# Turned attention heads: bank emptied by a ScalarE copy and divided on GpSimd instead of VectorE

## The reference

```python
xn = _layernorm(x, axis=-1)
# attention: q, k with rotary embedding, 4 query heads for each key/value head
scores = jnp.einsum('bqhd,bkhd->bhqk', q, k) / jnp.sqrt(jnp.float32(D))
probs = jax.nn.softmax(scores.astype(jnp.float32), axis=-1)
s = jnp.einsum('bhqk,bkhd->bqhd', probs, v).reshape(B, S, E)
# gate: z + gamma * m with gamma from the norms of z and m (low rank), then silu
g = _silu(z + gamma * m)
x = x + s * g
```

## Time and profile before

| | us |
|---|---|
| median of 3 runs | 461.4 |
| lowest and highest | 460.72 and 463.13 |
| the profiled execution | 464.08 |
| span of the profiled execution | 462.3 |
| PE busy | 449.7 |
| VectorE (DVE) busy | 379.2 |
| ScalarE (ACT) busy | 302.3 |
| GpSimd (POOL) busy | 87.9 |

### The profile page before, as it was taken

How to read it: one execution, slowest core, us unless ns; L and a number is a source line. 1 busy time by engine, 2 the same in 40 slices (tenths; PEclk the granted TensorE clock), 3 DMA queues, 4 the chain that set the end, 5 groups by cost and what they waited for, 6 DMA issues and landing times.

```text
span 462.3 us, 8804 instructions
## 1 busy us (share of the span) xinstructions
PE 449.7 (97%) x3237; PEld 203.6 (44%) x3237; DVE 379.2 (82%) x639; ACT 302.3 (65%) x593; POOL 87.9 (19%) x159
## 2 busy tenths in 40 slices
PE   8898999999999999999999999999999999999995
PEld 3465343443444444444444444444444444433342
DVE  5553588888999999999999999999999999534422
ACT  2120001224888888888888888888888888745594
POOL 8463212434101000000100010010001001014442
PEclk9989599999899999999999999999999999999998
DMA  8979944444000000000000000000000000020011
GB/s 261 319 108 125 114 68 68 68 72 69 2 1 3 1 4 1 1 4 1 3 0 3 3 2 3 1 3 0 3 4 1 3 0 3 2 81 2 20 47 36
DMA packets 13364, 17.45 MB, mean 38 GB/s; under 512 B 3088, under 2 KB 7440, under 8 KB 13328
## 3 DMA queue, kind: packets, MB, share of 16 engines
q1 hardware_dynamic: 11808, 15.84, 18.3%
q10 hardware_dynamic: 1520, 1.12, 0.9%
HBM read 6.72 MB, written 2.10 MB: 19 GB/s over the span
## 4 chain that ended last, share of the span: by engine, by line
PE 88%; DMA 4%; SPq 3%; DVE 2%; ACT 1%; issue 1%; POOL 0%; DVEq 0%
PE st L947 34%; PE oT L901 29%; PE sm L840 8%; PE st L780 7%; PE sm L920 3%; DMA kA<-arena 2%; PE sm L911 2%; DMA idb_sb<-in_identb 2%; PE oT L780 2%; PE st L816 1%; SPq L281 1%; PE sm L923 1%; DVE negmax L638 1%; SPq L313 1%; SPq L287 1%
## 5 line engine op out<-in xcount | busy, mean ns | idle before, releaser
L570 ACT ACTIVATE arena<-st 128x512 f32<-128x512 f32 x512 | 266.9, 600 | 56.5 <-PE st L947 53.5
L646 DVE TENSOR_REDUCE neghalf<-sm 128x1 f32<-128x512 f32 x448 | 270.7, 683 | 2.3 <-PE sm L840 0.4
L840 PE MATMUL sm<-kA,qA 48*128 48x512 f32 x512 | 187.7, 454 | 2.0 <-DMA kA<-arena 1.9
L947 PE MATMUL st<-qA,kA 50*128 50x512 f32 x512 | 177.9, 442 | 1.0 <-ACT arena L570 0.7
L901 PE MATMUL oT<-arena,vg 128*32 128x256 f32 (+3 forms) x1792 | 147.3, 421 | 0.0
L947 PEld LDWEIGHTS st<-qA,kA 50*128 50x128 f32 x512 | 84.2, 185 | 110.7 <-ACT arena L570 87.2
L840 PEld LDWEIGHTS sm<-kA,qA 48*128 48x128 f32 x512 | 85.9, 186 | 23.0 <-issue 14.0
L901 PEld LDWEIGHTS oT<-arena,vg 128*32 128x32 f32 x1792 | 38.7, 108 | 52.7 <-issue 42.2
L638 DVE TENSOR_REDUCE negmax<-sm 128x1 f32<-128x1024 f32 x32 | 38.1, 1221 | 15.9 <-PE sm L840 15.5
L409 POOL TENSOR_TENSOR maxp<-negmax,consts 128x16 bf16<-128x16 f32 x16 | 3.4, 214 | 214.2 <-DVE negmax L653 214.2
L497 ACT ACTIVATE arena<-arena 128x512 fp32r<-128x512 f32 x10 | 6.3, 630 | 57.7 <-POOL arena L369 57.7
(11 more groups left out here) (90 smaller groups left out, 259.6 us busy)
## 6 DMA issues: line engine op xcount, KB each, us to landing
qA<-arena SPq DMA_DIRECT2D x48, 128.0 KB, 5.1
x_sb<-in_x SPq DMA_DIRECT2D x8, 256.0 KB, 5.7
kA<-arena SPq DMA_DIRECT2D x12, 128.0 KB, 6.8
wT_sb<-in_wT SPq DMA_DIRECT2D x1, 1024.0 KB, 9.1
out<-x_sb SPq DMA_DIRECT2D x1, 896.0 KB, 4.0
out<-x_sb SPq DMA_DIRECT2D x4, 224.0 KB, 2.0
z_sb<-in_wq SPq DMA_DIRECT2D x1, 768.0 KB, 10.6
wkv<-in_wk ACTq DMA_DIRECT2D x1, 256.0 KB, 4.1
```

The lines of the kernel that those rows point to most:

```text
L570: act.activation(probs[:, s % PB, h, :], st[:, (st_score(0, s, h) - late) % 3, :], ACT.Exp, scale=float(D) ** -0.5).then_inc(st_free, 1)
L646: dve.tensor_reduce(neghalf[:, e // 16, e % 16, j % 2:j % 2 + 1], sm[:, n % 4, :], AX.X, ALU.max, negate=True).then_inc(sm_free, count)
L840: pe.matmul(sm[:, n % 4, :], qA[rows, half, g // 2, h, qt * P:(qt + 1) * P], kA[rows, g // 2, kh * HALF:(kh + 1) * HALF], start=True, stop ...
L947: pe.matmul(st[:, n % 3, :], kA[rows, g // 2, kt * P:(kt + 1) * P], qA[rows, half, g // 2, h, :], start=True, stop=True).then_inc(st_full, 1)
```

## The change

In groups 0 to 6, ScalarE copies the bank of turned heads into a tile in SBUF (`turned`, the memory of `junk`), ahead of exponential 12 or 44, and adds to a new semaphore `turned_out`. GpSimd makes the reciprocals as a power of -1 and multiplies. VectorE goes from maximum 11 to 12 and from 43 to 44 with nothing between them, and adds two to `sm_free` after maximum 11 and 43, one of them for the bank of turned heads; the matmul that writes this bank next (of pair 15 or 47) waits for `turned_out`. In the last group VectorE goes on as before. ScalarE's groups 1 to 6 are written out.

```diff
+        turned = junk[:, :, :].rearrange("p a n -> p (a n)").bitcast(F32)
...
+            def scale_turned(n, to):
+
+                came = turned.rearrange("p (t h c) -> p t h c", t=TH, h=REP)
+                sums = rsum[:, :].rearrange("p (t h) -> p t h", t=TH)
+                pool.wait_ge(turned_out, n + 1)
+                pool.tensor_tensor(sums, came[:, :, :, D], consts[:, 2:3].unsqueeze(2).broadcast_to((P, TH, REP)),
+                                   ALU.pow).then_inc(sums_inv, 1)
+                pool.wait_ge(sums_inv, n + 1)
+                pool.tensor_tensor(to.rearrange("p t (h d) -> p t h d", h=REP), came[:, :, :, 0:D],
+                                   sums.unsqueeze(3).broadcast_to((P, TH, REP, D)), ALU.mult).then_inc(heads_scaled, 1)
...
             def step(g, first=False):
                 if not first:
                     group_values(g)
+                    scale_turned(2 * g - 1, late_heads[:, :, (g - 1) * (REP * D):g * (REP * D)])
                 maxima(0, 2 * g + 3, 2 * g + 1,
                        (pj_full, PJ_AT["max0", 0] + 1) if first else (st_full, st_max0(g - 1) + 1))
+                scale_turned(2 * g, scaled[:, :, :])
...
+            def copy_turned(n, at):
+
+                act.wait_ge(sm_full, at + 1)
+                act.wait_ge(heads_scaled, n)
+                act.activation(turned, sm[:, at % 4, :], ACT.Copy).then_inc(turned_out, 1)
...
+                        if 4 * s + h == OUT1_AT and not first and not last:
+                            copy_turned(2 * g - 1, sm_out1(g))
+                        if 4 * s + h == OUT0_AT and not last:
+                            copy_turned(2 * g, sm_out0(g))
...
-            with act.Fori(1, LAST) as g:
+            for g in range(1, LAST):
                 step(g)
...
                 for j in range(64):
                     if j == 33:
                         both_halves(g, 0)
-                    if j == OUT1_AT and not first:
-                        hold_heads(g - 1, sm_out1(g), 1)
-                    if j == OUT0_AT:
-                        scale_heads(sm_out0(g), 1, 2 * g, scaled[:, :, :], None if first else g)
-                    row_max(g, j, 2 if first and j == OUT1_AT - 1 else 1)
+                    row_max(g, j, 2 if j in (OUT1_AT - 1, OUT0_AT - 1) else 1)
...
+                    if i == OUT1_AT + 3 and not first and not last:
+                        pe.wait_ge(turned_out, 2 * g)
+                    if i == OUT0_AT + 3 and not last:
+                        pe.wait_ge(turned_out, 2 * g + 1)
```

More of the change, by code:

```diff
@@ L252, in build @@
             "heads_out", "sums_inv", "heads_scaled", "heads_gated", "group_done"))
+        turned_out = sem("turned_out")
         late_copied, late_scaled, late_added = sem("late_copied"), sem("late_scaled"), sem("late_added")
@@ L689, in scale_heads @@
             def scale_heads(at, banks, n, to, done):
-                turned = sm[:, at % 4, :].rearrange("p (t h c) -> p t h c", t=TH, h=REP)
+                bank = sm[:, at % 4, :].rearrange("p (t h c) -> p t h c", t=TH, h=REP)
                 dve.wait_ge(sm_full, at + banks)
+                dve.wait_ge(heads_scaled, n)
                 if done is not None:
                     dve.wait_ge(group_done, done)
-                dve.reciprocal(rsum[:, :].rearrange("p (t h) -> p t h", t=TH), turned[:, :, :, D]).then_inc(sums_inv, 1)
+                dve.reciprocal(rsum[:, :].rearrange("p (t h) -> p t h", t=TH), bank[:, :, :, D]).then_inc(sums_inv, 1)
                 dve.wait_ge(sums_inv, n + 1)
-                dve.tensor_tensor(to.rearrange("p t (h d) -> p t h d", h=REP), turned[:, :, :, 0:D],
+                dve.tensor_tensor(to.rearrange("p t (h d) -> p t h d", h=REP), bank[:, :, :, 0:D],
                                   rsum[:, :].rearrange("p (t h) -> p t h", t=TH).unsqueeze(3)
```

## The result

The changed kernel takes 455.28 us (median of 4 runs, 454.3 to 456.25), the kernel before 461.06 in the same comparison (460.28 to 463.13). The ratio is 0.9868, with a 95% interval of 0.9829 to 0.9907: 5.8 us faster, where 5.7 were forecast. The sum came out; one of its terms did not, as the experiments show.

A forecast was written before the change was run, and what follows sets the result against it. VectorE's chain was taken to bound the loop; earlier maxima gain 6 x (0.43 + 0.44) + 0.46 = 5.7 us, with other costs counted as hidden, taking the 461.4 us median to 455.7 us, range 452.5 to 458.9.

The forecast's parts named there:

- VectorE bounds the loop: Loop of the kernel before: VectorE's chain alone explains the 40.4 us period, though PE and ScalarE are close.
- has almost no hole: VectorE in one loop turn before the change: measured busy 40.10 of 40.5 us, so almost no idle time.
- What is late next: At the turned heads: maximum 12 must wait for pair 12 until 204.50, so 0.43 us gained, 0.48 idle.
- rival 1: VectorE's reciprocals and products: the whole 12.1 us comes back, giving 449.3 us; chance 0.08.
- The period: One loop turn: 39.6 us forecast after the change, with 0.43 and 0.44 us gained at its two places.
- I see neither a gain nor a loss in it: ScalarE's groups 1 to 6 written out instead of looped: counted as no effect on time.
- ScalarE's copy: Copy ahead of exponential 12: falls in ScalarE's idle 0.88 us, delays it 0.06; costed at nothing, 0.8 kept for the range.
- Rivals 2 and 3: ScalarE or PE takes over, 462.1 or 458.9 us, chance 0.12; copy delays exponential 12, 467.8 us, chance 0.04.
- One sign of being wrong: PE's waits for ScalarE's exponentials, 66.9 us before: growth by several us would show the forecast wrong.
- The new wait of PE: PE's matmul of pairs 15 and 47 also waits for the copy: cost zero, with 1.1 us of cover.
- GpSimd: Power of 16 elements 3.2 us and product 0.73 us per turn, hidden in GpSimd's idle time: cost zero.
- rival 4: GpSimd's product comes too late for the next copy: a power of 19.5 us would give 468.7 us; chance 0.01.

## Why the prediction was right

**VectorE bounds the loop.** Right, with a small correction. The kernel before doesn't care where the reciprocal and the product lie (period 40.28 at both places), and the changed one doesn't care how much VectorE does in the gap. But "has almost no hole" was not quite true: about 0.1 us of each gap of 0.91 and 0.96 us was a wait for the turned heads, hidden under the end of a maximum, as the written-out loop shows.

**What is late next.** The step that decided the size was to ask when pair 12 can be reduced, and to read it from the exponential of the same pair. It gave a gap of 1.08 us between maxima 11 and 12 and an idle time of 0.4; measured are 1.05 and 0.36. The full 12.1 us of rival 1 did not come.

**The period.** 0.87 us were forecast for it. The move of the division gave 40.28 - 39.45 = 0.83 and the loop written out 0.19, together 1.01. So the prediction's sentence on ScalarE's written-out loop, "I see neither a gain nor a loss in it", is the step that failed, by 0.19 us a group, 1.1 us in all; the division was over-estimated by 0.04 a group. In the loop the gain is 6.5 us and not 5.7, of which the division is 5.4 (from the first to the last `both_halves` it is 261.25 us with only the loop written out, and 255.90 after the change). That the medians differ by 5.8, within 0.1 us of the forecast, is partly luck: the interval of the ratio, 0.9829 to 0.9907, is a gain of 4.3 to 7.9 us, and holds both, so the medians alone would not have shown the missing term. The failed step rested on exponential 44 alone, which is not late in the hardware loop; the delay of `evacuate` and of exponential 32 shows only beside a kernel with the loop written out.

**ScalarE's copy.** Cost nothing, right: none of 13 x 0.06 us was passed on (39.45 with and without). Rivals 2 and 3 had the price wrong too: even a second copy costs 0.13 and not 0.49 at a place. One sign of being wrong did come in part: PE's waits for exponentials grew by 3.5 us over the loop (66.9 to 70.4). The copies are not the reason, since without them it is 69.9 us, and the loop became shorter all the same.

**The new wait of PE** is nowhere in the view of waits. Right.

**GpSimd.** The power takes 2.91 us where 3.2 were estimated from one and two elements, the product 0.62 where 0.73 was taken. Both are hidden, and so is a second power; rival 4 is far off. The advice of the Trainium skill, "GPSIMD Engine Reference", section "Engine selection", to leave elementwise work on VectorE did not decide here: power and product take 2.91 and 0.62 us on GpSimd, reciprocal and product 0.26 and 0.42 on VectorE, and only VectorE's lay on the path.

## What to carry to other kernels

When the bounding engine is relieved, ask which input it will wait for next, and read the arrival time from another engine that uses the same matmul: this gave the half that was gained and the half that turned into idle time. Then move that input: here two constants took another 4.8 us (455.28 to 450.52; 4.15 of it between the first and the last `both_halves` of the profiles), more than four fifths of what the change itself had brought. And treat a loop in hardware or written out as part of the change: written out it was worth 1.1 us in the kernel before, and a hardware loop with two groups in its body cost 6.6 in the changed one.

## What was not expected of the hardware

- In a hardware loop ScalarE took up some waits later: the copy of `oT` 1.21 to 1.22 us after the start of its block instead of 1.13 to 1.14, exponential 32 0.60 us after its matmul instead of 0.54. Others, exponentials 12 and 44, were not late.
- A hardware loop on ScalarE with two groups in its body lost 2.8 us at each jump back; with one group nothing of the kind is seen. About half of it came after ScalarE's hole: PE had stood still for 1.14 us and ran at a granted clock of 0.50 for about 3 us.
- A minimum of two SBUF inputs of 128x16 on VectorE took 0.57 us instead of 0.17 when GpSimd added two SBUF tiles at the same time, while maxima of 512 elements out of PSUM kept their 0.598 us beside GpSimd's power, product and sums.
- GpSimd's power takes 0.59 us for 1 element, 0.76 for 2 and 2.91 for 16.
